# Attention's rows stored in the output, and the down projection added onto them in DRAM by accumulating transfers

## The reference

```python
x = x + xattn(_layernorm(x), ctx_1024, ...)        # 16 heads of 64, context of 64 rows
x = x + ffn(_layernorm(x), clip_x, clip_down, w_gate, w_up, w_down)

def ffn(x, clip_x, clip_down, w_gate, w_up, w_down):
    xq = _act_fake_quant(x, clip_x[0])             # one scale for the whole tensor
    gate = einsum("bsh,ih->bsi", xq, _weight_fake_quant(w_gate))   # i = 1408
    up = einsum("bsh,ih->bsi", xq, _weight_fake_quant(w_up))
    h = _act_fake_quant(silu(gate) * up, clip_down[0])             # again one scale: needs max |h| of all rows
    return einsum("bsi,hi->bsh", h, _weight_fake_quant(w_down))
```

## Time and profile before

| | us |
|---|---|
| median of 3 runs (lowest, highest) | 1291.38 (1291.06, 1292.88) |
| the profiled execution | 1291.84 |
| its span, first to last instruction | 1290.0 |
| PE busy in the span | 1254.6 (97%) |
| DVE busy | 1110.9 (86%) |
| ACT busy | 802.1 (62%) |
| POOL busy | 288.0 (22%) |

### The profile page before, as it was taken

How to read it: one execution, slowest core, us unless ns; L and a number is a source line. 1 busy time by engine, 2 the same in 40 slices (tenths; PEclk the granted TensorE clock), 3 DMA queues, 4 the chain that set the end, 5 groups by cost and what they waited for, 6 DMA issues and landing times.

```text
span 1290.0 us, 20436 instructions
## 1 busy us (share of the span) xinstructions
PE 1254.6 (97%) x7563; PEld 586.0 (45%) x7607; DVE 1110.9 (86%) x2117; ACT 802.1 (62%) x1211; POOL 288.0 (22%) x227
## 2 busy tenths in 40 slices
PE   6999799999999999999999999999999999989998
PEld 4644344444444444444444444444444444434443
DVE  7776979887988988898889868899999999889998
ACT  6588576587567757755875671334334334499993
POOL 2103421441343144224413420000000000012223
PEclk9999899999999999999999999999999999999999
DMA  8285146356246265462563391387656742399997
GB/s 302 77 242 172 34 115 212 87 149 208 73 131 205 72 187 135 115 212 67 163 215 97 98 272 60 87 280 265 228 205 260 251 141 70 111 340 418 420 418 303
DMA packets 182436, 241.74 MB, mean 187 GB/s; under 512 B 122032, under 2 KB 141248, under 8 KB 169920
## 3 DMA queue, kind: packets, MB, share of 16 engines
q1 hardware_dynamic: 182336, 240.43, 56.2%
HBM read 120.86 MB, written 90.57 MB: 164 GB/s over the span
## 4 chain that ended last, share of the span: by engine, by line
PE 78%; ACT 8%; DMA 7%; DVE 5%; issue 2%; SPq 1%; POOL 0%; DVEq 0%
PE pg L1586 11%; PE pu L1592 11%; PE po L77 9%; PE po L79 9%; PE po L78 9%; PE ring L79 7%; PE ring L77 7%; PE ring L78 7%; ACT hb L1450 4%; PE ring L1055 2%; PE ring L1082 2%; DMA out_dram<-xqT 2%; DMA out_dram<-xa 1%; DMA x<-in_x_dram 1%; DMA xqT<-x_rows_d 1%
## 5 line engine op out<-in xcount | busy, mean ns | idle before, releaser
L1428 ACT ACTIVATE sg<-pg,gate_scale 128x512 f32<-128x512 f32 x176 | 120.9, 687 | 183.5 <-PE pg L1586 183.5
L77 PE MATMUL ring<-yT,M 128*128 128x512 f16 x512 | 194.1, 379 | 0.0
L78 PE MATMUL ring<-yT,M 128*128 128x512 f16 x512 | 194.0, 379 | 0.0
L79 PE MATMUL ring<-yT,M 128*128 128x512 f16 x512 | 194.0, 379 | 0.0
L77 PE MATMUL po<-VW,p 128*128 128x512 f16 x480 | 182.9, 381 | 1.5 <-DVE p L667 1.5
L78 PE MATMUL po<-VW,p 128*128 128x512 f16 x480 | 182.4, 380 | 0.0
L79 PE MATMUL po<-VW,p 128*128 128x512 f16 x480 | 182.4, 380 | 0.0
L1586 PE MATMUL pg<-xqT,w 128*128 128x512 bf16 x690 | 178.8, 379 | 1.8 <-ACT xqT L1439 0.8
L1592 PE MATMUL pu<-xqT,w 128*128 128x512 bf16 x689 | 178.6, 379 | 0.8
L469 ACT ACTIVATE p<-E 128x512 f16<-128x512 f32 x120 | 75.0, 625 | 129.3 <-DVE E L663 129.3
L1502 DVE TENSOR_TENSOR hb<-pu,sg 128x512 f32<-128x512 f32 x176 | 120.9, 687 | 26.5 <-PE pu L1592 25.0
(11 more groups left out here) (238 smaller groups left out, 1991.0 us busy)
## 6 DMA issues: line engine op xcount, KB each, us to landing
hidden<-hb SPq DMA_DIRECT2D x11, 2816.0 KB, 9.1
xa<-x_rows_d SPq DMA_DIRECT2D x28, 1024.0 KB, 5.7
hb<-hidden SPq DMA_DIRECT2D x22, 1024.0 KB, 16.1
x<-in_x_dram SPq DMA_DIRECT2D x16, 1024.0 KB, 6.2
value_fold<-E SPq DMA_DIRECT2D x64, 256.0 KB, 2.5
VW<-value_fold SPq DMA_DIRECT2D x16, 1024.0 KB, 5.9
x_rows_d<-x SPq DMA_DIRECT2D x16, 1024.0 KB, 4.1
out_dram<-xa SPq DMA_DIRECT2D x11, 1024.0 KB, 12.8
```

Of the source, the lines that this page charges most:

```text
L77: nc.tensor.matmul(out, a_hi, b_hi, start=first, stop=False)
L78: nc.tensor.matmul(out, a_hi, b_lo, start=False, stop=False)
L79: return nc.tensor.matmul(out, a_lo, b_hi, start=False, stop=last)
L1428: nc.scalar.activation(sg[:, n % 4], pg[n % 4][:], ACT.Silu, scale=gate_scale[:, n % FT:n % FT + 1]).then_inc(silus, 1)
```

## The change

Attention's rows are stored straight into the output tensor: `x1_d` becomes a view of `out`, so that the feed-forward network's input is also loaded from there. In the down stage nothing loads the rows again. `scale_down` writes its product into `xa[slot]` rather than `sg`, and waits for nothing but the sums and, from q = 4 on, the landing of the transfer that last read that buffer. Both adds are gone. POOL issues one transfer for each block that reads `xa[slot]` and adds it onto the output's rows in DRAM (`accum_op=ALU.add`); for the last block there are four, one for each t. SP's queue keeps only the loads of hidden values.

```diff
-        def load_r(q):
-            slot = (2 + q) % 4
-            wait(sp, out_stored[slot], 16 * (q // 4))
-            sp.dma_start(xa[slot], x1_d[taken_as(q)]).then_inc(r_loaded[slot], 16)
...
         load_h(5)
-        for q in range(NG):
-            if q + 6 < NG:
-                load_h(q + 6)
-            slot = (2 + q) % 4
-            if q < NG - 1:
-                sp.wait_ge(added, 2 * q + 2)
-                sp.wait_ge(added_too, 2 * q + 2)
-                sp.dma_start(og[taken_as(q)], xa[slot]).then_inc(out_stored[slot], 16)
...
-            if 0 < q < NG - 3:
-                load_r(q + 3)
+        for q in range(6, NG):
+            load_h(q)
...
+        for slot in range(4):
+            pool.wait_ge(done["x1_stored"][slot], 16 * NG // 4)
         for q in range(NG):
             slot = (2 + q) % 4
-            pool.wait_ge(r_loaded[slot], 16 * (q // 4) + 16)
-            for t in range(2):
-                pool.wait_ge(down_taken, 4 * q + t + 1)
-                nc.gpsimd.tensor_tensor(xa[slot][:, t], xa[slot][:, t], sg[:, t], ALU.add).then_inc(added, 1)
+            if q < NG - 1:
+                pool.wait_ge(down_taken, 4 * q + TT)
+                nc.gpsimd.dma_start(og[taken_as(q)], xa[slot], accum_op=ALU.add).then_inc(out_stored[slot], 16)
+            else:
+                for t in range(TT):
+                    pool.wait_ge(down_taken, 4 * q + t + 1)
+                    nc.gpsimd.dma_start(og[taken_as(q)][:, t], xa[slot][:, t], accum_op=ALU.add).then_inc(out_stored[slot], 16)
...
         def scale_down(q, t):
+            slot = (2 + q) % 4
+            if t == 0:
+                wait(dve, out_stored[slot], 16 * (q // 4))
             dve.wait_ge(downs, 4 * q + t + 1)
-            wait(dve, added if t < 2 else added_too, 2 * (q - 1) + t % 2 + 1)
-            nc.vector.tensor_tensor(sg[:, t], sums_of(q)[t][:], down[:], ALU.mult).then_inc(down_taken, 1)
-
-        def add_rows(q, t):
...
-            nc.vector.tensor_tensor(xa[slot][:, t], xa[slot][:, t], sg[:, t], ALU.add).then_inc(added_too, 1)
+            nc.vector.tensor_tensor(xa[slot][:, t], sums_of(q)[t][:], down[:], ALU.mult).then_inc(down_taken, 1)
...
-        x1_d = nc.dram_tensor("x1_rows_d", [NG, P, TT, D], fp32).ap()
+        x1_d = out.rearrange("b (j t p) d -> (b j) p t d", j=2, p=P)
```

More of the change, by code:

```diff
@@ L1284, in ffn @@
     h_loaded = [sem(f"h_loaded{k}") for k in range(5)]
-    r_loaded = [sem(f"r_loaded{k}") for k in range(4)]
     out_stored = [sem(f"out_stored{k}") for k in range(4)]
     down_scales, h_scaled, h_step, h_rounded = sem("down_scales"), sem("h_scaled"), sem("h_step"), sem("h_rounded")
-    downs, down_taken, added, added_too = sem("downs"), sem("down_taken"), sem("added_by_pool"), sem("added_by_dve")
+    downs, down_taken = sem("downs"), sem("down_taken")
     og = out.rearrange("b (j t p) d -> (b j) p t d", j=2, p=P)
@@ L1381, in on_sync @@
                 sp.dma_start(h_d[g], hb[:, HOME[g]]).then_inc(h_stored[HOME[g]], 16)
-        sp.wait_ge(ups, NG * FT)
-        load_r(0)
         for slot in range(2):
@@ L1386, in on_sync @@
         load_h(5)
-        for q in range(NG):
-            if q + 6 < NG:
-                load_h(q + 6)
-            slot = (2 + q) % 4
-            if q < NG - 1:
-                sp.wait_ge(added, 2 * q + 2)
-                sp.wait_ge(added_too, 2 * q + 2)
-                sp.dma_start(og[taken_as(q)], xa[slot]).then_inc(out_stored[slot], 16)
-            else:
-                for t in range(TT):
-                    if t < 2:
-                        sp.wait_ge(added, 2 * q + t + 1)
-                    else:
-                        sp.wait_ge(added_too, 2 * q + t - 1)
-                    sp.dma_start(og[taken_as(q)][:, t], xa[slot][:, t]).then_inc(out_stored[slot], 16)
-            if 0 < q < NG - 3:
-                load_r(q + 3)
+        for q in range(6, NG):
+            load_h(q)
         for k in range(4):
@@ L1569, in on_vector @@
                 scale_down(q, t)
-                if t >= 2 and not more:
-                    add_rows(q, t)
-            if more:
-                add_rows(q, 2)
-                add_rows(q, 3)
     def on_tensor(pe):
```

9 lines of the change are left out of this document (removed).

## The result

| | before | changed |
|---|---|---|
| median of the runs taken together, us | 1291.77 | 1304.38 |
| lowest and highest, us | 1291.06 to 1292.88 | 1303.16 to 1305.22 |
| profiled execution, us | 1291.84 | 1304.24 |
| its span, us | 1290.0 | 1302.4 |

What follows compares the result with a forecast made beforehand. PE was taken to set the pace, with transfers nearly as much the bound. A 4.8 us gain was possible if DMA kept up; at x = 5.0 the end is 1299.5 + 1.84 - 0.5 = 1301 us, range 1286 to 1350.

Steps and rivals of the forecast that it cites:

- x: Down stage: time of all 16 DMA engines for one 1 MB accumulating transfer, bounded 2.5 to 9.8 us, taken as 5.0.
- the cheap case: Rival for the down stage: x up to 4.2 us costs nothing, PE-bound to the end, 1287 us; chance 0.27.
- the case without overlap: Rival: accumulates don't overlap their own parts, x above 5.6, DMA alone bounds from 1148 on, 1310 to 1367 us; chance 0.20.
- The two queues share the engines evenly: Down stage: accumulates of blocks 0 to 12 nearly done when block 15's hidden load lands, at 1209.2 + 13x, 1274.5.
- 0.5 at x = 5.0, which never reaches 28: Down stage: accumulate backlog grows 2x - 9.5 us a block, 0.5, never reaching the 28 us until its buffer is needed.
- The new wait on `out_stored`: Down stage: scaling waits for the accumulate four blocks earlier; no loss at x = 5.0, reached from about x = 5.8.
- its own sign: Sign of the 1301 us forecast: ACT idle ahead of blocks 13 to 15, waiting for hidden loads.
- at nothing: Attention and first stage: 16 stores to 2 KB pieces and 16 loads from there cost nothing, DMA being less than full.
- not on the path: Down stage: POOL's adds, 2.5 us a block, were not on the path, so removing them gains nothing.
- The 1.1 us at block 2: Start of the down stage: without DVE's adds the rounding for block 2 is 2 us earlier; PE gains 1.1 us.
- The tail: After PE's end: scaling 0.7, store 2.4, 1.0 more for the accumulate; at x = 5.0 the last landing is seen at 1299.5.
- POOL's issue and DVE: Rival for the down stage: POOL's issuing of transfers holds DVE's roundings, around 1322 us; chance 0.08.

Runs made afterwards that it cites:

- e2: The changed kernel with plain stores from POOL's queue in place of the adding transfers, so attention's rows are not added: 1291.82 us, ratio 0.9997 to the kernel before.
- e13: e10 with the third part of each of the 11 hidden loads left out, so the output differs: 1289.78 us, ratio 0.9980 to the kernel before.
- e15: e10 with each hidden load split by token tiles into pieces of 2 KB: 1315.19 us, ratio 1.0177 to the kernel before.
- e10: The changed kernel with one small POOL add of one column behind the all-reduces: 1301.26 us, ratio 1.0073 to the kernel before.
- e6: The changed kernel with blocks 0 to 3 and 15 done by row loads, engine adds and plain stores: 1289.18 us, ratio 0.9979 to the kernel before.
- e3: The kernel before with attention's rows kept in the output tensor in 2 KB pieces, adds and stores unchanged: 1295.13 us, ratio 1.0023.
- e12: e6 with all four residual adds of blocks 0 to 3 on POOL, none on DVE: 1292.49 us, ratio 0.9998 to the kernel before.
- e14: e12 with the rows of groups 10 to 14 in a tensor of their own, 8 KB pieces: 1291.44 us, ratio 0.9994 to the kernel before.

## Where the prediction was right, and where not

**The direction, and the size of x: right.** The adding transfer was the one unknown, bounded from 2.5 to 9.8 us and taken as 5.0. It is 5.07 (207 GB/s). The two bounds from the Trainium skill's page "Collectives: The Full Stack" (section "The bandwidth ceiling") bracket nothing here: its ratio of 1.93 gave 4.8 us, an estimate close to the measured value, and its figure for one engine gave 4.1 us, which these transfers didn't reach. Both the cheap case and the case without overlap are out. That a plain store in the same place costs nothing (e2) and that less other work brings all of the gain (e13) show that x works through the amount of DMA work, as the prediction had it.

**"The two queues share the engines evenly": wrong.** This was the step from x to the place of the loss. The queues in the stretch from 1150 to 1240 (packets, MB, share of 16 engines):

```profile
q1 hardware_dynamic: 3386, 22.71, 64.3%
...
q0 software_dynamic: 3371, 6.71, 40.9%
```

SP's hidden loads (q1) got 64% of the engines and moved 22.7 MB; POOL's adding transfers (q0) got 41% and moved 6.7 MB, 6.4 transfers of 1 MB in 9.5 blocks. Even were the packets (3386 and 3371), not the bytes. The hidden loads were all there by 1257, nearly 12 us ahead of their use at 1268.76, and ACT never waited for them; the prediction had it wait 15.8 us. The adding transfers piled up instead. With it fell "0.5 at x = 5.0, which never reaches 28": 6.4 in 90 us is one in 14 us, so the backlog grew by 4.6 us a block and not by 0.5. Block 3's transfer is the first that comes too late:

```profile
1174.24 1.87 POOL L1395 DMA_DIRECT2D out_dram<-xa  x1 [7.26 <-DVE xa L1530]
```

It landed at 1210.2, 36 us after its issue, and DVE had been ready for its buffer (block 7) after 33.8. Block 6's took 49.8. The new wait on `out_stored`, priced at nothing at x = 5.0, is where the loss sits. The prediction had named that wait as the sign of a transfer that doesn't overlap its own parts (x above 5.6); it came at x = 5.07, so the sign doesn't tell that case from an uneven sharing. And its own sign, ACT idle ahead of blocks 13 to 15, did not come. It comes in e15, where both queues get nearly equal bytes: there ACT waits 26.4 us and DVE doesn't.

**The clock: not in the sum.** After the waits ahead of blocks 11 and 12 the granted clock was 0.79 and 0.58 in two stretches and two blocks lost 1.66 and 1.75 us, 3.4 together. The prediction priced idle time of TensorE at its length alone. In e10 three blocks run 10.35, 10.28 and 10.35 us (for 40 products, otherwise 8.87) after such waits. A lower clock does not follow each wait: block 2 has the same 1.25 and 0.75 us of them in the kernel before and in e6, and only in e6 did it slow down.

**The layout, "at nothing": right for this change.** The step looked at attention and the first stage, where DMA has room, and e3 and e10 show 0.7 us at most there. The 3 us that e3 lost lie in the down stage, where it still loads rows; the changed kernel loads none there.

**Ahead of the stage: 3.4 us that no step had.** The prediction took POOL's adds as "not on the path" and looked only at what they cost in time. Their removal also took away the instruction ahead of them, and POOL's start came 7 us later; one add put back takes this away (e10).

**The 1.1 us at block 2: about right.** 0.9 measured, for the reason given: the rounding is earlier and the block's last part is late next.

**The tail: right in kind, 2.8 us missing.** From TensorE's end, the prediction has 4.1 us if transfers keep up (0.7 + 2.4 + 1.0), and 7.4 us in its forecast, where block 14's transfer is issued at 1287.7 and two transfers' worth of work follows it in the queue. The trace has 6.5 us, but with TensorE's end later; the queue's own times tell more. Block 14's transfer is issued at 1287.44. In 40 slices of 0.4 us, from 1287 to 1303, the engines moved:

```profile
GB/s 41 31 10 41 0 46 51 0 159 195 174 174 164 205 205 215 205 210 200 210 205 205 200 210 200 210 200 210 200 210 190 195 205 174 21 0 0 0 0 0
```

They begin at 1290.2 and work until about 1300.8 on the 2.1 MB of blocks 14 and 15, as forecast (10 us); the landing is seen 1.6 us later (forecast 1.8). What the sum lacked is the 2.8 us from the start of POOL's issue to the first data. POOL's last issue shows part of it:

```profile
1296.94 0.87 POOL L1399 DMA_DIRECT2D out_dram<-xa  x1 [1.28 <-DVE xa L1530]
```

The scaling ends at 1296.64 and the issue at 1297.8; the transfer is seen at the end of the span, 1302.4, 4.6 us later, where a whole store took 2.4 from its issue.

**The sum.** The forecast was 1301, and 1304.4 was measured; e10, which lacks the start delay, gave 1301.3. This agreement is partly luck: the forecast had TensorE's end at 1292.1 by one long wait of ACT, and the trace has it at 1295.9 by four waits of DVE, with 3.4 us of start delay and 3.4 of clock in it. The amount of DMA work was right; the path on which it reached TensorE was another one.

**The rivals.** POOL's issue and DVE: refuted as a cause (roundings of 1.35 against 1.22 us), though the two engines do exclude each other beside POOL's adds, both in the kernel before and in e12, as the Trainium skill's page "SBUF — State Buffer" (section "Who interferes with whom") has it for shared ports. Its rule for transfers that GpSimd issues shows here in the issue: 1.87 us beside roundings, 1.28 us where DVE rounds nothing.

```profile
1287.44 1.28 POOL L1395 DMA_DIRECT2D out_dram<-xa  x1 [7.63 <-DVE xa L1530]
```

0.6 us of an issue and 0.1 us of a rounding are what the two cost each other in a block, and beside them TensorE's blocks 3 to 8 follow each other at 9.50 us.

## What to carry to other kernels

A transfer that adds in DRAM costs the DMA engines twice a plain store here. It takes work from the vector engines and gives it to the queue, so it pays only for those blocks for which the queue has room, and not for the last one, whose landing is on the path; the best version used it for 11 of 16 blocks. Where two queues compete for full engines, don't assume even shares of bytes: here they got even numbers of packets, so the queue with the larger pieces got more bytes. Ask for either what waits if it is late. And when an engine's last work of a kind is removed, look at which compiler-made instructions go with it.

## What the runs showed of the hardware

- Adding transfers of 1 MB in 2 KB pieces, alone in the queue: 207 GB/s, 5.07 us of all 16 engines; plain ones 409 to 420 GB/s in a full queue. One of 256 KB lands after 5.8 us (2.4 plain).
- With work in both SP's and POOL's queue, the engines took as many packets of each: 3386 and 3371 with pieces of 6.7 and 2.0 KB (22.7 and 6.7 MB), 463 and 464 with pieces of 2 KB in both (e15, 1203 to 1210). The shares of the engines' time were 64% and 41% in the first case; they count packets in flight and add up to more than 100%.
- POOL spends 1.87 us on issuing an adding transfer of 1 MB in 2 KB pieces beside DVE's roundings, 1.28 without them; a plain one 1.14 (e2). In the tail the first data moved 2.8 us after the start of an issue.
- In a kernel whose last POOL work after the all-reduces is no ordinary operation, POOL's first affine select comes 7 us later, of which about 3 us reached the end of this kernel. One add of a column behind the all-reduces takes this away (e10).
- TensorE lost 1.4 to 2.9 us a block to a lower granted clock, after idle times of 0.8 to 2.9 us, in some executions and not in others: block 2 after 1.83 us of them took 11.77 us for 40 products in e12 and 8.88 in e14.
